# A graph-network kernel: bank and wait value of every visit written out in a 16 bit table instead of packed codes

## Chip, core and metric

One core of a Trainium2 chip. The metric is the device time of one execution in microseconds, the median of the runs shown; lower is better.

## What is computed

Four graph layers follow each other on 3125 nodes with 64 features and 103,125 edges, each behind a layer norm and a ReLU, each added to x. `src` and `dst` are sorted by `dst`. Cut to what matters here:

```python
def reference(x, src, dst, edge_attr_32, edge_attr_64, edge_weight, ...):
    h = relu(layernorm(x)); x = x + L0(h, src, dst)          # 10 hops: segment_sum of (h * norm)[src] by dst
    h = relu(layernorm(x)); x = x + L1(h, (src, dst), edge_weight)   # 3 weighted graph convolutions
    h = relu(layernorm(x)); x = x + L2(h, (src, dst), edge_attr_32)  # attention over edges
    h = relu(layernorm(x)); x = x + L3(h, edge_attr_64, src, dst)    # messages, mean by dst, output
    return x
```

The 13 propagations of L0 and L1 run as products with dense matrices of 3125 x 3125. One of edge counts stays on the chip, one of summed edge weights goes to memory. The change is in how these two matrices are built.

## The kernel before

The program is a row of stages. In each stage every engine has its own instruction stream, and all engines meet at its end. `stage_tables` makes index tables (to 87 us of the profiled execution), `stage_build` builds the two matrices (to about 790 us), then come the hops, the convolutions, attention and messages, which the change leaves as they are.

**Visits.** The 806 tiles of 128 edges (`TB`) meet 392 blocks of 8 destination nodes (`BB`). Because the edges are sorted by `dst`, tiles and blocks are walked together in V0 = 1197 visits: each visit adds one tile's share to one block. For a visit TensorE multiplies one-hot rows (`rows`: source within its 128, once plain and twice times the high and low part of the weight) by one-hot columns (`cols`: node chunk and destination), with 226, 200 and 200 columns (L486, L487, L488). The sums lie in PSUM, the tensor `banks`; block j has bank j mod 8. Visits are made in 120 batches of ten (`TP`) and on TensorE in 240 groups of five (`GV`).

**Who makes what.** VectorE makes the one-hot rows and columns of a batch in five passes: L447, L448, L449 and twice L452. There are two slots for batches, so VectorE begins batch b when all visits up to batch b-2 are done (`vis_done`), and TensorE begins a batch when its one-hots are ready (`oh_ready`). GpSimd copies table values for a batch (L429). ScalarE takes each finished pair of blocks: it copies two banks of sums (L512), zeroes the banks of the pair before (L517, which counts up `freed`), and casts the counts to their place (L519); the pair to take is given by a table of last visits, loaded at L522. SyncE stores the weight sums (L536).

**The codes.** Which bank a visit adds to is known only on the chip. `stage_tables` packs for each group of five visits one 32 bit code: three bits of bank for each visit, and nine bits with the newest block of the group (`JBITS`, `JMAX`, L329 to L339, written to `vis`). In the build stage all 1197 visits are written out for TensorE one after the other, without a loop. Every eighth group (a leg, 40 visits) it loads eight codes into registers (`codes`, L472), each checked against its range. `group` waits for `freed` with a value unpacked from the code (L481), and for each visit takes its bank out by a shift and a mask:

```python
                pe.wait_ge(freed, ((x & (JMAX - 1)) >> 1) + 1)
                for u in range(n):
                    t = GV * half + u
                    bank = (x >> (JBITS + 3 * u)) & (BANKS - 1)
```

These operations on registers are instructions of TensorE's sequencer, which also issues the weight loads and matmuls in program order. The trace names them ALU_OP, FUSED_REGOPS, SEQ_ASSERT (the check) and TENSOR_LOAD (the load of registers).

Of the kernel before, what the change touches and what calls it, by code (L numbers as in the profile page):

```python
# [9 lines left out]
BF16 = mybir.dt.bfloat16  # L10
I32 = mybir.dt.int32
I16 = mybir.dt.int16
ALU = mybir.AluOpType
ACT = mybir.ActivationFunctionType
X = mybir.AxisListType.X
# [25 lines left out]
J0 = NDST // BB  # L41
V0 = T0 + J0 - 1
V0P = 1280
TP = 10
NBATCH = -(-V0 // TP)
GV = 5
NG5 = -(-V0 // GV)
VT = NBATCH * TP
CW = NCH * BB
CAW = CW + NCH + 1  # L50
BANKS = 8
JBITS = 9
JMAX = 1 << JBITS
ROW, COL, CHUNK, WHI, WLO = range(5)
VISW = 640

# [7 lines left out]
GROUP = DC // P  # L64
WDOWN = 2.0 ** -10
NDC = -(-NDST // DC)
BLOCK1, ENDS, BLOCK2 = 0, 32, 96
R = 8
RT = 64
NWORDS = V2P // 4  # L70
# [32 lines left out]
class Mem:  # L103


    def __init__(self, nc, ctx):
# [10 lines left out]

        self.vis = sb("vis", [P, VISW], I16)
        scales = sb("scales", [P, 2], F32)
        self.scale, self.unscale = scales[:, 0:1], scales[:, 1:2]  # L120
        self.ident = sb("ident", [P, P], F32)
        self.iotaH = sb("iotaH", [P, CW], F16)
        self.colsN = sb("colsN", [P, 8, NCH], F32)
# [11 lines left out]
        self.landed_e = [sem(f"landed_e{i}") for i in range(R)]  # L135
        self.landed_q = [sem(f"landed_q{i}") for i in range(R)]

    def steps(self):

        return self.vis[BLOCK1:BLOCK1 + 1, :].bitcast(I32)[:, 0:NG5]  # L140

    def ends(self):

# [2 lines left out]
    def tabs5(self):  # L146

        return self.work[:, 0:5 * VT // 2].bitcast(F16).rearrange("p (k v) -> p k v", k=5)

# [24 lines left out]
def stage_tables(nc, m, last0, last, dst, src, edges):  # L174
# [4 lines left out]
    with ExitStack() as ctx:  # L179
        sem = lambda n: ctx.enter_context(nc.semaphore(n))  # L180
        raw = m.big
        at = [0]

        def take(n):
            at[0] += n
            return raw[:, at[0] - n:at[0]]
# [8 lines left out]
                tI=take(C).bitcast(I32), blkF=take(C), tF=take(C), end=take(C), cmp=take(C * VP // 2).bitcast(BF16).rearrange("p (c v) -> p c v", c=C),  # L195
                tv=take(VP), tvc=take(VP), jv=take(VP + 2), tcol=take(K).bitcast(I32)))
        cmpJ = take(C0 * J0 // 2).bitcast(BF16).rearrange("p (c j) -> p c j", c=C0)
        ends, steps = take(J0), take(NG5)
        r1 = take(K1 * 3 * TB).bitcast(I32).rearrange("p (k a e) -> p k a e", k=K1, a=3)
        r2 = take(K2 * 2 * TE).bitcast(I32).rearrange("p (k a e) -> p k a e", k=K2, a=2)  # L200
        f1 = take(K1 * 4 * TB).rearrange("p (k a e) -> p k a e", k=K1, a=4)
# [3 lines left out]
        valid, tmp = m.work2[:, 0:V0P], m.work2[:, V0P:2 * V0P]  # L205
        jI = m.work2[:, 2 * V0P:3 * V0P].bitcast(I32)
# [12 lines left out]
        for arr in range(4):  # L219
            for k in range(0, K1, 4):  # L220
                n = min(4, K1 - k)
# [16 lines left out]
        def _(po):  # L238
            po.iota(iotaI, pattern=[[1, V0P]], base=0, channel_multiplier=0).then_inc(s_iota, 1)
            for s in schemes:  # L240
                po.iota(s["tI"], pattern=[[P, s["C"]]], base=0, channel_multiplier=1).then_inc(s_iota, 1)
            po.memset(m.ident[:, :], 0.0).then_inc(s_pool, 1)
            po.wait_ge(s_pool, 1)
            po.affine_select(out=m.ident[:, :], in_=m.ident[:, :], compare_op=ALU.not_equal, fill=1.0, base=0,
                             pattern=[[-1, P]], channel_multiplier=1).then_inc(s_iota, 1)
# [46 lines left out]
        def _(dve):  # L292
            chain = m.dve_step.on(dve)
            chain(dve.memset(onesB, 1.0))
            dve.wait_ge(s_iota, 4)
            chain(dve.tensor_copy(iotaF, iotaI))
            chain(dve.tensor_copy(m.iotaH[:, :], iotaI[:, 0:CW]))
            dve.wait_ge(s_last, 32)
            for s in schemes:
                chain(dve.tensor_scalar(s["blkI"], s["lastI"], s["shift"], None, ALU.arith_shift_right))  # L300
                chain(dve.tensor_copy(s["blkF"], s["blkI"]))
                chain(dve.tensor_copy(s["tF"], s["tI"]))
                chain(dve.tensor_tensor(s["end"], s["blkF"], s["tF"], ALU.add))
                for c in range(s["C"]):
                    ins = dve.tensor_scalar(s["cmp"][:, c, :], iotaF[:, 0:s["VP"]], s["end"][:, c:c + 1], None, ALU.is_gt)
                ins.then_inc(s_cmp, 1)
            for c in range(C0):
                ins = dve.tensor_scalar(cmpJ[:, c, :], iotaF[:, 0:J0], schemes[0]["blkF"][:, c:c + 1], None, ALU.is_ge)
            ins.then_inc(s_cmp, 1)
            for n, s in enumerate(schemes):  # L310
                dve.wait_ge(s_tv, n + 1)
                for q in range(s["VP"] // s["chunk"]):
                    part = slice(q * s["chunk"], (q + 1) * s["chunk"])
                    ins = dve.tensor_copy(s["tv"][:, part], m.PB[s["banks"] + q][:, 0:s["chunk"]])
                chain(ins)
                chain(dve.tensor_tensor(s["jv"][:, 1:s["VP"] + 1], iotaF[:, 0:s["VP"]], s["tv"], ALU.subtract))
                dve.tensor_scalar(s["tvc"], s["tv"], float(s["T"] - 1), None, ALU.min).then_inc(s_tvs, 1)
            for n, s in enumerate(schemes):
                dve.wait_ge(s_tc, n + 1)
                for g in range(-(-s["K"] // 4)):  # L320
                    k = min(4, s["K"] - 4 * g)
# [5 lines left out]
            j1 = schemes[0]["jv"][:, 1:V0P + 1]  # L327
            dve.wait_ge(s_tvs, 2)
            chain(dve.tensor_scalar(valid, j1, float(J0 - 1), None, ALU.min))  # L329
            chain(dve.tensor_copy(jI, valid))  # L330
            chain(dve.tensor_scalar(jI, jI, BANKS - 1, None, ALU.bitwise_and))
            chain(dve.tensor_copy(tmp, jI))
            five = tmp[BLOCK1:BLOCK1 + 1, 0:GV * NG5].rearrange("p (k u) -> p k u", u=GV)
            newest = valid[BLOCK1:BLOCK1 + 1, 0:GV * NG5].rearrange("p (k u) -> p k u", u=GV)[:, :, GV - 1]
            code = steps[BLOCK1:BLOCK1 + 1, :]
            chain(dve.scalar_tensor_tensor(code, five[:, :, GV - 1], float(BANKS), five[:, :, GV - 2], ALU.mult, ALU.add))
            for u in range(GV - 3, -1, -1):
                chain(dve.scalar_tensor_tensor(code, code, float(BANKS), five[:, :, u], ALU.mult, ALU.add))
            chain(dve.scalar_tensor_tensor(m.steps(), code, float(JMAX), newest, ALU.mult, ALU.add))  # L339

            dve.wait_ge(s_tv, 3)
            chain(dve.tensor_scalar(ends, m.PB[6][:, 0:J0], float(T0 - 1), 1.0, ALU.min, ALU.add))
# [22 lines left out]
            chain(dve.scalar_tensor_tensor(valid, chT, 1.0, valid, ALU.add, ALU.mult))  # L365
            dve.tensor_scalar(m.tab(COL), tmp[:, 0:VT], -1.0, None, ALU.add)
            dve.tensor_scalar(m.tab(CHUNK), valid[:, 0:VT], -1.0, None, ALU.add)
            chain(dve.tensor_copy(m.tab(ROW), rowT[:, 0:VT]))

# [6 lines left out]
            chain(dve.tensor_scalar(wT, wT, m.scale, None, ALU.mult))  # L376
            chain(dve.tensor_copy(m.tab(WHI), wT[:, 0:VT]))
            chain(dve.tensor_tensor(m.tab(WLO), wT[:, 0:VT], m.tab(WHI), ALU.subtract))

# [14 lines left out]
def stage_build(nc, m, aw):  # L394

    with ExitStack() as ctx:
# [3 lines left out]
        slots = []  # L400
        for home in (m.work[:, free:free + size], m.work2[:, 0:size]):
            h16 = home.bitcast(F16)
            rows = h16[:, 0:3 * TP * P].rearrange("p (i t r) -> p i t r", i=3, t=TP)
# [12 lines left out]
        oh_ready = sem("build_oh")  # L416
        vis_done = sem("build_visit")
        freed = sem("build_freed")
# [5 lines left out]
        @block.gpsimd  # L424
        def _(po):
            for b in range(NBATCH):
                if b >= 2:
                    po.wait_ge(oh_ready, b - 1)
                po.tensor_copy(twice[b % 2], m.tabs5()[:, :, b * TP:(b + 1) * TP].unsqueeze(3).to_broadcast([P, 5, TP, 2])).then_inc(doubled, 1)  # L429

        @block.vector
        def _(dve):
# [5 lines left out]
            def batch(b, k, first=False):  # L438
# [8 lines left out]
                dve.tensor_tensor(pairwise(rows[:, 0, :, :]), iota(P), value(ROW, P), ALU.is_equal).then_inc(rows_ready, 1)  # L447
                dve.tensor_tensor(pairwise(cols[:, :, 0:CW]), iota(CW), value(COL, CW), ALU.is_equal)  # L448
                dve.tensor_tensor(pairwise(cols[:, :, CW:CAW]), iota(CAW - CW), value(CHUNK, CAW - CW), ALU.is_equal)  # L449
                dve.wait_ge(rows_ready, b + 1)  # L450
# [13 lines left out]
            chain = m.dve_step.on(dve)  # L464
            chain(dve.tensor_copy(dout, m.PS[:, 0, 2 * CW:2 * CW + NCH]))
            for b in range(1, BANKS):
                chain(dve.tensor_tensor(dout, dout, m.PS[:, b, 2 * CW:2 * CW + NCH], ALU.add))

        @block.tensor
        def _(pe):  # L470
            def codes(g, n):
                _, xs = nc.values_load_multi_w_load_instructions(m.steps()[:, bass.ds(g, n)], [mybir.EngineType.PE], min_val=0,  # L472
                                                                 max_val=JMAX * BANKS ** GV - 1)
                return xs

            def group(x, b, half, k, n=GV):

                rows, cols = slots[k]
                if half == 0:
                    pe.wait_ge(oh_ready, b + 1)  # L480
                pe.wait_ge(freed, ((x & (JMAX - 1)) >> 1) + 1)  # L481
                for u in range(n):
                    t = GV * half + u
                    bank = (x >> (JBITS + 3 * u)) & (BANKS - 1)
                    to = lambda c0, c1: m.PS[:, bass.ds(bank, 1), c0:c1].rearrange("p b c -> p (b c)")
                    pe.matmul(to(CW, CW + CAW), rows[:, 0, t, :], cols[:, t, :], start=False, stop=True, skip_group_check=True)  # L486
                    pe.matmul(to(0, CW), rows[:, 1, t, :], cols[:, t, 0:CW], start=False, stop=True, skip_group_check=True)  # L487
                    pe.matmul(to(0, CW), rows[:, 2, t, :], cols[:, t, 0:CW], start=False, stop=True, skip_group_check=True).then_inc(vis_done, 1)  # L488

            pe.wait_ge(init, 1)  # L490
            for b in range(BANKS):
                ins = pe.matmul(m.PS[:, b, 0:CW + CAW], blank[:, 0, 0:P], blank.rearrange("p t c -> p (t c)")[:, 0:CW + CAW], start=True, stop=True)
                if b % 2:
                    ins.then_inc(freed, 1)
            for g in range(NG5):
                if g % 8 == 0:
                    xs = codes(g, min(8, NG5 - g))
                group(xs[g % 8], g // 2, g % 2, g // 2 % 2, min(GV, V0 - g * GV))

        @block.scalar  # L500
        def _(act):
# [1673 lines left out]
```

## Time and profile before

| | us |
|---|---|
| median of 3 runs | 3705.48 |
| lowest and highest | 3702.94, 3708.67 |
| the profiled execution, first to last instruction | 4103.0 |
| of it before the build stage | 87 |
| build stage | 703 |
| after it | 3313 |

The profiled execution is 398 us longer than the median of the timed ones. Its rows name engines as PE (TensorE's matmuls), PEld (its weight loads), PEldq (its sequencer), DVE (VectorE), ACT (ScalarE), POOL (GpSimd) and SP (SyncE). Register instructions do not count as busy time; where an engine waited for nothing that the profile can name, the releaser reads "issue". Starts and ends are in us from the first instruction; the ends of matmuls are modelled, their starts are recorded. The granted clock is a share of TensorE's 2.4 GHz, 1.00 or 0.50 at any moment.

### The profile page before, as it was taken

How to read it: one execution, taken by the hardware profiler on the slowest of the kernel's cores; microseconds unless marked ns; L12 is line 12 of the kernel's file. 1: busy time of each engine (PE TensorE's matmuls, PEld its weight loads, DVE VectorE, ACT ScalarE, POOL GpSimd, SP SyncE). 2: the span in 40 equal slices, each digit the busy share in tenths (PEclk: the TensorE clock that was granted, in tenths of full speed). 3: DMA queues.
4: the chain of work that ended last, by engine and by line, in shares of the span. 5: the costliest groups of instructions: out<-in, count | busy, mean ns of one | idle time of the engine just before them, and what ended most of it. 6: DMA issues, size and time to landing. Idle time of an engine off the chain costs nothing. (4 is left out here: it accounts for less than half of the span.)

```text
span 4103.0 us, 80080 instructions
## 1 busy us (share of the span) xinstructions
PE 3139.2 (77%) x17480; PEld 1972.5 (48%) x17480; DVE 1986.4 (48%) x6935; ACT 1606.3 (39%) x4621; POOL 1627.3 (40%) x1766
## 2 busy tenths in 40 slices
PE   3788788879997797577777777777866778787877
PEld 2444444444443343455566656556643444444445
DVE  6656666556656115344444444444673444444442
ACT  1555555413322001233333333333453444444445
POOL 2000000024333001666666666666106666666660
PEclk7899898999998998687777777877977888888885
DMA  1111111125557995322222222222112222222220
GB/s 38 57 59 57 57 59 59 51 93 193 188 177 261 406 360 185 65 54 55 54 55 54 55 54 53 54 55 54 40 28 56 66 63 66 64 66 63 66 61 13
DMA packets 417722, 370.64 MB, mean 90 GB/s; under 512 B 175608, under 2 KB 342232, under 8 KB 417336
## 3 DMA queue, kind: packets, MB, share of 16 engines
q1 hardware_dynamic: 365912, 315.65, 23.8%
q0 software_dynamic: 46144, 48.98, 6.5%
q8 instruction: 198, 3.24, 0.3%
q10 hardware_dynamic: 5280, 1.23, 0.1%
q14 instruction: 188, 1.54, 0.1%
HBM read 279.65 MB, written 86.00 MB: 89 GB/s over the span
## 5 line engine op out<-in xcount | busy, mean ns | idle before, releaser
L1451 POOL DMA_INDIRECT big<-row_table,src x806 | 761.5, 945 | 487.3 <-issue 183.4
L1870 POOL DMA_INDIRECT big<-message_table,src x610 | 612.0, 1003 | 394.5 <-DVE big L2000 172.1
L1476 PE MATMUL banks<-big 97*128 x902 | 399.8, 534 | 148.6 <-issue 138.1
L1492 PE MATMUL banks<-big 128*128 x1804 | 349.0, 326 | 174.8 <-ACT big L1508 110.1
L486 PE MATMUL banks<-work 128*128 128x226 f16 x1197 | 350.3, 293 | 138.6 <-issue 131.0
L1492 PEld LDWEIGHTS banks<-big 128*128 128x128 f32 x1804 | 312.4, 244 | 202.5 <-issue 202.1
L1909 PE MATMUL banks<-big 128*128 128x512 f16 x1225 | 395.6, 441 | 4.4 <-DVE big L1988 4.4
L850 PE MATMUL banks<-big,work 128*128 128x512 f16 (+1 forms) x1750 | 352.1, 359 | 22.3 <-DVE work L984 17.4
L1541 DVE TENSOR_REDUCE big<-banks 128x1 f32<-128x256 f32 x451 | 189.4, 420 | 332.5 <-PE banks L1476 183.8
L1508 ACT COPY big<-banks 128x256 f32<-128x256 f32 x451 | 169.8, 377 | 439.5 <-remote 194.0
L1918 PEld LDWEIGHTS banks<-big 128*64 128x64 f32 x1804 | 173.8, 164 | 343.6 <-issue 343.0
L1918 PE MATMUL banks<-big 128*64 x1804 | 247.5, 268 | 116.5 <-issue 98.3
L487 PE MATMUL banks<-work 128*128 128x200 f16 x1197 | 335.6, 280 | 0.0
L488 PE MATMUL banks<-work 128*128 128x200 f16 x1197 | 326.9, 273 | 0.0
L429 POOL COPY work<-work 128x100 f16<-128x100 f16 x120 | 35.9, 300 | 666.9 <-DVE work L452 649.9
L1558 DVE SCALAR_TENSOR_TENSOR big<-big,banks 128x97 f32 x451 | 142.4, 316 | 325.0 <-remote 208.5
L486 PEld LDWEIGHTS banks<-work 128*128 128x128 f16 x1197 | 121.9, 102 | 363.1 <-issue 350.1
L512 ACT ACTIVATE work<-banks 128x800 f32<-128x800 f32 x196 | 164.3, 838 | 330.6 <-PE banks L488 330.6
L908 POOL TENSOR_TENSOR work<-work 128x400 f16<-128x400 f32 x196 | 180.1, 946 | 284.8 <-DVE work L977 244.2
L2006 DVE TENSOR_SCALAR big<-big 128x512 f16<-128x512 f16 x1225 | 281.6, 285 | 2.3
L2000 DVE TENSOR_TENSOR big<-banks,big 128x128 f32<-128x128 f32 x305 | 87.3, 286 | 399.8 <-remote 257.3
L1476 PEld LDWEIGHTS banks<-big 97*128 97x128 f32 x902 | 177.4, 244 | 198.9 <-issue 196.4
(338 smaller groups left out, 5835.8 us busy)
## 6 DMA issues: line engine op xcount, KB each, us to landing
big<-weights_halves SPq DMA_DIRECT2D x16, 6400.0 KB, 20.8
weights_dense<-work SPq DMA_DIRECT2D x196, 200.0 KB, 1.9
work<-weights_dense SPq DMA_DIRECT2D x196, 200.0 KB, 2.7
weights_halves<-work SPq DMA_DIRECT2D x98, 400.0 KB, 2.6
big<-q_table SPq DMA_DIRECT2D x451, 64.0 KB
big<-in_ef SPq DMA_DIRECT2D x403, 64.0 KB
big<-in_ea SPq DMA_DIRECT2D x403, 32.0 KB
big<-row_table,src POOLq DMA_INDIRECT x806
```

The lines of the kernel that those rows point to most:

```text
L486: pe.matmul(to(CW, CW + CAW), rows[:, 0, t, :], cols[:, t, :], start=False, stop=True, skip_group_check=True)
L487: pe.matmul(to(0, CW), rows[:, 1, t, :], cols[:, t, 0:CW], start=False, stop=True, skip_group_check=True)
L488: pe.matmul(to(0, CW), rows[:, 2, t, :], cols[:, t, 0:CW], start=False, stop=True, skip_group_check=True).then_inc(vis_done, 1)
L850: ins = pe.matmul(m.PB[c % 4][:, 0:width(c)], z[k][:, a, :, :], counts[:, a, c * DC:c * DC + width(c)], start=(a == 0), stop=(a == NCH - 1))
L1451: po.indirect_dma_start(rows[:, t % RT, s, 0:D], None, x_t.rearrange("a p c -> (a p) c"), bass.IndirectOffsetOnAxis(ap=m.src2[:, s, t:t + ...
L1476: pe.matmul(psS[v % 2], qT[v % R][0:XW, :], XF[0:XW, bass.ds(slot, 1), :].rearrange("p t e -> p (t e)"), start=False, stop=True).then_inc( ...
L1492: ins = pe.matmul(psA[v % 2], PT[v % 2][:, s * P:(s + 1) * P], rows[:, bass.ds(slot, 1), s, :].rearrange("p t c -> p (t c)"), start=(s == ...
L1541: dve.tensor_reduce(rm[s3], psS[i % 2], op=ALU.max, axis=X, negate=True).then_inc(s_small, 1)
L1870: po.indirect_dma_start(G[n % R][:, s, :], None, g_t.rearrange("a p c -> (a p) c"), bass.IndirectOffsetOnAxis(ap=m.src2[:, s, t:t + 1], ax ...
L1909: pe.matmul(psH[q % 2], table[:, a, :, :].rearrange("p s d -> p (s d)"), hot[n % HOT], start=(a == 0), stop=(a == NCH - 1)).then_inc(hot_u ...
L1918: ins = pe.matmul(psA[v % 4], oh[v % 4][:, s, :], M[:, bass.ds(slot, 1), s, :].rearrange("p t c -> p (t c)"), start=(s == 0), stop=(s == 1))
L2006: dve.tensor_scalar(hot[n % HOT], key[q % 2], float(P * a - CENTER), None, ALU.is_equal).then_inc(hot_ready, 1)
```

## The change

Instead of one packed code for each five visits, `stage_tables` writes a table of 16 bit numbers. For each leg, now 20 visits, it holds 20 offsets into PSUM (bank times 512) and 4 wait values, one for each group of five, ready for use. 60 legs of 24 numbers lie in two rows of `work` (partitions 0 and 32), in columns that nothing else of the build stage uses. TensorE loads 24 registers a leg with one instruction, with no check of range, adds a constant to the offset for the column, and has no shift, mask or unpacking left.

```diff
+LEG = 2 * TP
+NLEG = VT // LEG
+WALK = LEG + LEG // GV
+WALK_AT = 6160
+BOUNDED = "the table is written from values that are clamped when it is made"
...
+WALK_ROWS = (0, 32)
...
-    def steps(self):
-
-        return self.vis[BLOCK1:BLOCK1 + 1, :].bitcast(I32)[:, 0:NG5]
+    def walk(self, half):
+
+        n = NLEG // 2 * WALK
+        row = WALK_ROWS[half]
+        return self.work[row:row + 1, WALK_AT:WALK_AT + n // 2].bitcast(I16)
+
+    def leg(self, g):
+
+        half, at = divmod(g, NLEG // 2)
+        return self.walk(half)[:, at * WALK:(at + 1) * WALK].bitcast(U16)
...
+            pairI = tmp.bitcast(I32)
             chain(dve.tensor_copy(jI, valid))
+            chain(dve.tensor_scalar(pairI, jI, 1, None, ALU.arith_shift_right))
             chain(dve.tensor_scalar(jI, jI, BANKS - 1, None, ALU.bitwise_and))
-            chain(dve.tensor_copy(tmp, jI))
-            five = tmp[BLOCK1:BLOCK1 + 1, 0:GV * NG5].rearrange("p (k u) -> p k u", u=GV)
-            newest = valid[BLOCK1:BLOCK1 + 1, 0:GV * NG5].rearrange("p (k u) -> p k u", u=GV)[:, :, GV - 1]
-            code = steps[BLOCK1:BLOCK1 + 1, :]
-            chain(dve.scalar_tensor_tensor(code, five[:, :, GV - 1], float(BANKS), five[:, :, GV - 2], ALU.mult, ALU.add))
-            for u in range(GV - 3, -1, -1):
-                chain(dve.scalar_tensor_tensor(code, code, float(BANKS), five[:, :, u], ALU.mult, ALU.add))
-            chain(dve.scalar_tensor_tensor(m.steps(), code, float(JMAX), newest, ALU.mult, ALU.add))
+            n = VT // 2
+            for half, row in enumerate(WALK_ROWS):
+                to = m.walk(half).rearrange("p (g w) -> p g w", w=WALK)
+                part = lambda v: v[row:row + 1, half * n:(half + 1) * n]
+                chain(dve.tensor_scalar(to[:, :, 0:LEG], part(jI).rearrange("p (g v) -> p g v", v=LEG), 512, None, ALU.mult))
+                newest = part(pairI).rearrange("p (g q u) -> p g q u", g=NLEG // 2, u=GV)[:, :, :, GV - 1]
+                chain(dve.tensor_scalar(to[:, :, LEG:WALK], newest, 1, None, ALU.add))
...
+            flat = m.PS[:, :, :].rearrange("p b c -> p (b c)")
+
+            def leg(g):
+                _, xs = nc.values_load_multi_w_load_instructions(m.leg(g), [mybir.EngineType.PE], min_val=0, max_val=(BANKS - 1) * 512,
+                                                                 skip_runtime_bounds_check_because=BOUNDED)
+                return xs[0:LEG], xs[LEG:WALK]
+
+            def batch(b, places, needed):
+
+                rows, cols = slots[b % 2]
+                pe.wait_ge(oh_ready, b + 1)
+                for t in range(min(TP, V0 - b * TP)):
+                    if t % GV == 0:
+                        pe.wait_ge(freed, needed[t // GV])
+                    to = lambda c0, c1: flat[:, bass.ds(places[t] + c0, c1 - c0)]
                     pe.matmul(to(CW, CW + CAW), rows[:, 0, t, :], cols[:, t, :], start=False, stop=True, skip_group_check=True)
...
-            for g in range(NG5):
-                if g % 8 == 0:
-                    xs = codes(g, min(8, NG5 - g))
-                group(xs[g % 8], g // 2, g % 2, g // 2 % 2, min(GV, V0 - g * GV))
+            for g in range(NLEG):
+                places, needed = leg(g)
+                for u in range(2):
+                    batch(2 * g + u, places[u * TP:(u + 1) * TP], needed[u * (TP // GV):(u + 1) * (TP // GV)])
```

TensorE's program where the first leg of the build stage begins, before the change:

```order
L472 TENSOR_LOAD vis
L472 ISA x16
L481 REGISTER_ALU [waits build_oh]
L481 ISA
L486 REGISTER_ALU [waits build_freed]
L486 REGISTER_ALU
L486 ISA
L486 MATMUL banks<-work 128x226
L487 ISA
L487 MATMUL banks<-work 128x200
L488 MATMUL banks<-work 128x200
```

The same place in the changed kernel (L486 is now the load of a leg; L498, L499 and L500 are the three matmuls):

```order
L486 TENSOR_LOAD work
L498 ISA [waits build_freed,build_oh]
L498 MATMUL banks<-work 128x226
L499 ISA
L499 MATMUL banks<-work 128x200
L500 MATMUL banks<-work 128x200
```

The sixteen instructions behind the load, the two of L481 and the two REGISTER_ALU are gone, and both waits stand on one register instruction. There are 30 such loads before and 60 now.

TensorE's program where one group of five ends and the next begins within a batch, before:

```order
L488 MATMUL banks<-work 128x200
L481 REGISTER_ALU
L481 ISA
L486 REGISTER_ALU [waits build_freed]
L486 REGISTER_ALU
L486 ISA
L486 MATMUL banks<-work 128x226
```

and in the changed kernel:

```order
L500 MATMUL banks<-work 128x200
L498 ISA [waits build_freed]
L498 MATMUL banks<-work 128x226
```

Between two visits of one group there are `L486 REGISTER_ALU x2` and `L486 ISA` before, and `L498 ISA` alone now. VectorE's program in `stage_tables`, before:

```order
L332 CAST work<-work 128x1280
L336 SCALAR_TENSOR_TENSOR big<-work 1x240
L338 SCALAR_TENSOR_TENSOR big<-big,work 1x240 x3
L339 SCALAR_TENSOR_TENSOR vis<-big,work 1x240
L342 TENSOR_SCALAR big<-banks 128x392
```

and now:

```order
L344 TENSOR_SCALAR work<-work 128x1280
L349 TENSOR_SCALAR work<-work 1x30x20
L351 TENSOR_SCALAR work<-work 1x30x4
L349 TENSOR_SCALAR work<-work 1x30x20
L351 TENSOR_SCALAR work<-work 1x30x4
L354 TENSOR_SCALAR big<-banks 128x392
```

One pass of a single row less stands there, and the pass over 1280 columns is a mask in place of a cast. The programs of the other engines keep their instructions and their order.

## Rows read from the trace of the kernel before

**Rows 1.** the build stage by engine: busy us (instructions), clock, DMA share, GB/s
```profile
core 0: us, PE busy (x) PEld busy (x) DVE busy (x) ACT busy (x) POOL busy (x), PEclk, DMA share, GB/s
...
87.00:790.00 703.00, 561.62 (x3591) 297.67 (x3591) 430.28 (x602) 395.79 (x587) 35.23 (x118) 0.90 0.16 58
```

**Rows 2.** who waited for whom, 87 to 790: us in all, times, longest
```profile
PEld banks L486 <- issue: 350.1, 958, 3.7
...
DVE work L447 <- PE banks L488: 265.2, 118, 5.3
...
PE banks L486 <- ACT banks L517: 6.2, 24, 0.4
```

**Rows 3.** timeline of TensorE: start and length of loads (PEld) and matmuls (PE)
```profile
400.63 0.10 PEld L486 LDWEIGHTS banks<-work 128*128 128x128 f16 x1 [0.22 <-issue]
...
400.75 0.26 PE L487 MATMUL banks<-work 128*128 128x200 f16 x1
400.76 0.10 PEld L488 LDWEIGHTS banks<-work 128*128 128x128 f16 x1
400.85 0.25 PE L488 MATMUL banks<-work 128*128 128x200 f16 x1
401.08 0.10 PEld L486 LDWEIGHTS banks<-work 128*128 128x128 f16 x1 [0.22 <-issue]
...
402.22 0.25 PE L488 MATMUL banks<-work 128*128 128x200 f16 x1
...
402.82 0.10 PEld L486 LDWEIGHTS banks<-work 128*128 128x128 f16 x1 [0.58 <-issue]
```

**Rows 4.** register instructions of lines 472 and 486: count, ns min/median/max
```profile
L472 PEldq TENSOR_LOAD <-vis x30: 587/591/867, 83.2 to 764.2; - x30
...
L486 PEldq ALU_OP  x2394: 36/36/36, 87.1 to 785.8; - x200
```

**Rows 5.** timeline of TensorE round the load of a leg
```profile
318.69 0.25 PE L488 MATMUL banks<-work 128*128 128x200 f16 x1
322.43 0.36 PE L486 MATMUL banks<-work 128*128 128x226 f16 x1 [3.49 <-issue]
```

**Rows 6.** columns of rows 1, for the 5.5 us behind that load
```profile
322.40:327.90 5.50, 5.47 (x32) 4.54 (x33) 0.28 (x1) 2.97 (x5) 0.27 (x1) 0.50 0.10 37
```

**Rows 7.** other loads of registers: two by line 1230, four by line 522
```profile
L1230 PEldq TENSOR_LOAD <-vis x114: 7/537/727, 1650.6 to 4064.2; - x114
...
L522 ACTq TENSOR_LOAD <-vis x49: 304/307/513, 83.2 to 777.1; - x49
```

**Rows 8.** timeline of VectorE in a batch, then of ScalarE in a pair
```profile
402.59 0.83 DVE L447 TENSOR_TENSOR work<-iotaH,work 128x1280 f16<-128x1280 f16 x1 [1.40 <-PE banks L488]
...
404.65 1.55 DVE L452 TENSOR_TENSOR work<-work 128x1280 f16<-128x1280 f16 x2
...
402.06 0.84 ACT L512 ACTIVATE work<-banks 128x800 f32<-128x800 f32 x1 [1.27 <-PE banks L488]
402.79 0.83 ACT L517 COPY banks<-colsN 128x800 f32<-128x800 f32 x1
403.55 0.53 ACT L519 ACTIVATE big<-work 128x400 f32 x1
```

**Rows 9.** timeline where VectorE's first batch ends and TensorE begins
```profile
85.24 1.55 DVE L452 TENSOR_TENSOR work<-work 128x1280 f16<-128x1280 f16 x2
...
86.71 0.82 DVE L447 TENSOR_TENSOR work<-iotaH,work 128x1280 f16<-128x1280 f16 x1
...
87.42 0.10 PEld L486 LDWEIGHTS banks<-work 128*128 128x128 f16 x1 [1.96 <-issue]
```

**Rows 10.** a group of VectorE ahead of the stage, 20 to 62 us
```profile
L349 DVE TENSOR_SCALAR big<-big 128x128 int32<-128x128 int32 x10 | 2.2, 219 | 12.2 <-DMA big<-in_dst,big 12.0
```

**Rows 11.** the page: instructions in the trace, those of its busy groups
```profile
span 4103.0 us, 80080 instructions
...
PE 3139.2 (77%) x17480; PEld 1972.5 (48%) x17480; DVE 1986.4 (48%) x6935; ACT 1606.3 (39%) x4621; POOL 1627.3 (40%) x1766
```

More of the change, by code:

```diff
@@ L12 @@
 I16 = mybir.dt.int16
+U16 = mybir.dt.uint16
 ALU = mybir.AluOpType
@@ L46 @@
 GV = 5
-NG5 = -(-V0 // GV)
 VT = NBATCH * TP
+LEG = 2 * TP
[3 more added lines that the diff above has]
+BOUNDED = "the table is written from values that are clamped when it is made"
 CW = NCH * BB
@@ L51 @@
 BANKS = 8
-JBITS = 9
-JMAX = 1 << JBITS
 ROW, COL, CHUNK, WHI, WLO = range(5)
@@ L66 @@
 NDC = -(-NDST // DC)
-BLOCK1, ENDS, BLOCK2 = 0, 32, 96
+ENDS, BLOCK2 = 32, 96
+WALK_ROWS = (0, 32)
 R = 8
@@ L197, in stage_tables @@
         cmpJ = take(C0 * J0 // 2).bitcast(BF16).rearrange("p (c j) -> p c j", c=C0)
-        ends, steps = take(J0), take(NG5)
+        ends = take(J0)
         r1 = take(K1 * 3 * TB).bitcast(I32).rearrange("p (k a e) -> p k a e", k=K1, a=3)
@@ L470, in _ @@
         def _(pe):
[L471 to L485, printed above, removed]
+            flat = m.PS[:, :, :].rearrange("p b c -> p (b c)")
[10 more added lines that the diff above has]
+                    to = lambda c0, c1: flat[:, bass.ds(places[t] + c0, c1 - c0)]
                     pe.matmul(to(CW, CW + CAW), rows[:, 0, t, :], cols[:, t, :], start=False, stop=True, skip_group_check=True)
```

## The prediction, made before the changed kernel ran

> **What bounds the kernel now.** Read the stretches first [rows 1]: the build stage, which the change touches, lasts from 87 to 790 us, 703 of 4103 us, and no other stretch runs lines that it edits, except some short passes of VectorE before 87. In the stage no engine is full: VectorE is busy 430 us, ScalarE 396 us, GpSimd 35 us. TensorE reads as busy 562 us, but the ends of its matmuls are modelled. Then the waits of the stage [rows 2]: VectorE waits 265 us for TensorE's L488, and TensorE waits for almost nobody (6.2 us for ScalarE). What stands before L486 is "issue", 350.1 us on the weight loads in 958 pieces, so TensorE's own sequencer sets the pace.
>
> The timeline of single visits shows what it does there [rows 3]. Weight loads of L486 start at 400.63 and 401.08: a visit takes 0.45 us. From the load of L486 to L487, where one register instruction stands, 0.12 us pass; from the load of L488 (400.76) to the next of L486, where three stand (two ALU_OP, one FUSED_REGOPS), 0.32 us. The two ALU_OPs (the shift and the mask, 2394 in all [rows 4]) thus cost 0.32 - 0.12 = 0.20 us a visit. Where a group of five ends, the wait value is unpacked too: from the matmul of L488 to the next load are 0.60 us (402.22 to 402.82) and not 0.23 (400.85 to 401.08), 0.37 more. Where a leg of eight groups ends, the load of eight codes, its sixteen check instructions and the unpacking hold TensorE from a matmul at 318.69 to one at 322.43 [rows 5], 3.74 us.
>
> Together: 957 visits inside groups at 0.465 (0.45, and 0.52 in the slow stretches) are 445 us; 29 pauses at 3.74 are 108 us; the remaining 150 us on 210 group ends are 0.71 each.
>
> **The change part by part, in the time of the profiled execution.**
>
> *Visits.* Without two ALU_OPs the sequencer needs 0.45 - 0.20 = 0.25 us. Now the matmuls themselves count: at the half clock, granted 0.50, 32 matmuls start in 5.5 us [rows 6], a visit of three in 0.52, so they need 0.26 at the full one; the distance of 0.10 from L487 to L488 at full clock [rows 3], where nothing but the matmul holds, gives up to 0.30 for three. I take 0.28: 957 x 0.28 = 268 us.
>
> *Group ends.* The unpacking at L481 goes, and the wait stands on the first register instruction of the group. The wait costs something still: I take 0.1 us over a visit, between nothing and the 0.37 of [rows 3]. 240 x 0.38 = 91 us.
>
> *Loads.* 60 loads of 24 registers replace 30 of eight, without checks. A load of eight took 0.591 us, one of two on the same sequencer 0.537 [rows 4, 7]: 0.009 a register, so 24 make 0.74, with decoding 0.8. The upper bound by rows is ScalarE's 0.307 for four [rows 7], 0.077 each, 1.84 for 24. I take 0.8, because the two rows of TensorE differ so little: 60 x 0.8 = 48 us.
>
> TensorE alone would then need 268 + 91 + 48 = 407 us, 3.4 a batch, in place of 703. It will not be alone.
>
> *VectorE* makes a batch in 3.53 us when nobody holds it: 3.61 from 402.59 to the end of L452 [rows 8], less the 0.08 by which the next batch can overlap it (86.79 and 86.71 [rows 9]). That is 424 us for 120, a floor which the change does not touch. The slots are two, so VectorE's batch b+1 waits for TensorE's b-1 and TensorE's b for VectorE's b. Round that ring two batches cost VectorE's time, TensorE's time and both hand-overs: from the last matmul (402.22, [rows 3]) to VectorE's start at 402.59 are 0.28 us beyond the visit; from VectorE's end at 86.79 to the first weight load at 87.42 were 0.63 [rows 9], of which four of five register instructions go, leaving 0.2. So (3.53 + 3.4 + 0.5) / 2 = 3.7 us a batch, 446 us in all.
>
> *ScalarE* needs 2.02 us for a pair of blocks, 402.06 to 404.08 [rows 8], 396 us for 196. It is below the ring, but only by a tenth, and pairs do not come evenly; with a remainder of slow clock I add 4%: 465 us. The stores take a DMA share of 0.16 [rows 1], which leaves room for a faster stage.
>
> *Clock.* The slow stretches follow the 3.74 us pauses: after the one at 318.69 it is 0.50 from 322.4 to 327.9 [rows 6]. With pauses of at most about a microsecond I expect it near 1, above the 0.90 of [rows 1].
>
> *Tables before the stage.* One pass over 1280 goes for another, and five small ones make way for four; all stand ahead of a wait of 12.0 us for an indirect DMA [rows 10]. They cost nothing; were that cover gone, it would be 1 us either way.
>
> Sum: 703 - 465 = 238 us less in the profiled execution. Behind the stage all engines meet, so it passes on whole.
>
> **From the profiled to the timed execution.** The profiled one took 4103 us, the median is 3705: recording cost 398 us somewhere, and the stage's own share must come off the gain. By span it has 703 / 4103 of it, 68 us. By instructions: the trace has 80,080, of which 48,282 are counted as busy [rows 11]; of the other 31,798, TensorE's sequencer has some 5,750 here (30 x 16, 240 x 2, 1197 x 4), 18%, and double that if half of them elsewhere hide behind others: 144 us. I take 100 us. The timed stage is then about 603 before; after, VectorE's instructions hold it near 453, as few register instructions are left. The gain is 150 us: 3705 - 150 = 3555 us.
>
> **Rivals.**
>
> *Recording costs the stage nothing.* Then the 238 us are whole: 3467 us. For it: matmuls and VectorE's passes look untouched by it. Against it: 398 us must lie somewhere, and register work is what this stage is made of. 15%.
>
> *ScalarE takes the ring.* If freeing a pair of banks comes late for TensorE (the wait at a group's first visit asks for the newest of five blocks), 196 pairs cost 2.02 us plus 0.5 of hand-over, 494 us, and the timed gain is near 110 to 120; with the larger share of recording, 75: 3630 us at the end. For it: a pair's banks come free only behind the 0.84 us pass of the next pair and their own zeroing. Against it: 6.2 us of such waits now. 18%.
>
> *The clock falls and stays.* At 1.2 GHz a batch takes 10 x 0.52 + 0.2 + 0.4 = 5.8 us, 696 us, against 603 timed before: 93 us slower, 3798 us. It decides from the point where a batch passes 5.0 us, that is with the half clock in about seven tenths of the stage. For it: a mean of 0.90 in the stage, so half clock in a fifth of it today. Against it: these stretches follow pauses that go. 4%.
>
> *The load is dear per register.* If 24 registers cost in proportion and not 0.009 us each, the loads grow. By ScalarE's 0.077 [rows 7] a load takes 1.84 us, a batch of TensorE 0.52 more and one round the ring 0.26 more: 31 us, 3586 us, inside the forecast. It ends on the slower side only where TensorE's batch passes 603 / 120 = 5.0 us, 2.8 + 0.2 + 2.0, with a load over 4 us. Rows with eight registers in 0.591 us [rows 4] speak against it: 2%. The Trainium skill, page Runtime: NRT & Kernel Launch, The ~15µs preamble/postamble breakdown and the notes on TENSOR_LOAD, gives about 200 ns a register for loads from HBM, in bulk too; by that a load here would be 4.8 us, the stage 10 x 0.28 + 0.2 + 2.4 = 5.4 us a batch, 648 us, and the kernel 3750. The trace disagrees for this one from SBUF, at 74 ns a register with eight.
>
> *It does not take the two instructions away.* The row of TensorE's order has one in their place; if that one grew to 0.3 us, the time would stand. 2%.
>
> **How the numbers follow.** The forecast, 3500 to 3600, has 57%; the first two rivals 15% and 18%; the last three 8%; 2% for anything else. The range, 3460 to 3635, holds the first three. About 0.2% (7 us) is what a measurement can tell from no change. Faster 0.93, same 0.02, slower 0.05.
>
> **What would show it.** Right: no ALU_OP and no SEQ_ASSERT in the visits; weight loads of L498 0.26 to 0.30 us apart in a batch; a load of some 0.75 us; VectorE's wait at its first operation of a batch down from 265 us to under 50; granted clock near 1; the stage 440 to 500 us in the profile. Wrong: the stage at 470 in the profile and the timed gain far from 150 (then the share of recording was off); ScalarE's zeroing as a releaser of TensorE with tens of us; a clock of 0.5 through whole slices; or a gap of over 1 us at each load.

## The result, and the profile after

The changed kernel takes 3763.74 us (median of 4 runs, 3756.19 to 3768.96) against 3706.15 before: a ratio of 1.015, interval 1.0135 to 1.0164. It is 58 us slower where 150 us less were forecast, and outside the range.

The profiled execution spans 3760.3 us, as long as the timed ones. The build stage lasts from 90 to 842 us, 752 us where [rows 1] had 703. Here is that stretch, in the columns of [rows 1]:

```profile
core 0: us, PE busy (x) PEld busy (x) DVE busy (x) ACT busy (x) POOL busy (x), PEclk, DMA share, GB/s
90.00:842.00 752.00, 455.72 (x3591) 407.82 (x3591) 425.19 (x594) 386.55 (x583) 113.66 (x118) 0.77 0.14 54
```

The same matmuls and the same passes of VectorE as before, but the granted clock is 0.77 and not 0.90. The waits in it (us in all, times, longest), which answer to [rows 2]:

```profile
ACT work L524 <- PE banks L500: 385.6, 126, 30.1
DVE work L459 <- PE banks L500: 319.3, 59, 6.3
PEld banks L498 <- issue: 312.5, 60, 6.3
PE banks L498 <- DVE work L464: 249.7, 51, 5.6
```

The waits of TensorE's weight loads for "issue" were 958, of 350 us in all; now they are 60, of 312 us, up to 6.3 us each. The many small gaps are gone and 60 long ones have come: one for each leg. VectorE waits for TensorE more than before, 319 us for 265. The row with 249.7 us lies inside the same gaps and names VectorE as releaser, but it is not what TensorE waited for: in the trace the first matmul of each of the 60 legs starts behind the end of its load, 0.27 us in the middle, and the one-hots of its batch had then been ready for 2.3 to 4.7 us. The load of a leg, in the columns of [rows 4]:

```profile
L486 PEldq TENSOR_LOAD <-work x60: 5847/6168/6443, 84.7 to 828.2; - x60
```

A load of 24 registers takes 6.17 us, not 0.74. What TensorE does round one of them, the answer to [rows 3] and [rows 5]:

```profile
302.47 0.25 PE L499 MATMUL banks<-work 128*128 128x200 f16 x1
302.56 0.25 PE L500 MATMUL banks<-work 128*128 128x200 f16 x1
302.64 0.26 PE L498 MATMUL banks<-work 128*128 128x226 f16 x1
302.74 0.25 PE L499 MATMUL banks<-work 128*128 128x200 f16 x1
302.82 0.25 PE L500 MATMUL banks<-work 128*128 128x200 f16 x1
307.80 0.37 PE L498 MATMUL banks<-work 128*128 128x226 f16 x1 [4.73 <-DVE work L464]
307.96 0.37 PE L499 MATMUL banks<-work 128*128 128x200 f16 x1
308.13 0.37 PE L500 MATMUL banks<-work 128*128 128x200 f16 x1
308.30 0.40 PE L498 MATMUL banks<-work 128*128 128x226 f16 x1
```

Ahead of the load visits follow each other every 0.27 us, as forecast (L500 at 302.56 and 302.82). Then nothing starts from 302.82 to 307.80. The one-hots that it needs next are ready at 304.12, the end of these two passes of VectorE (two more, which end at 307.72, are for the batch after):

```profile
302.57 1.55 DVE L464 TENSOR_TENSOR work<-work 128x1280 f16<-128x1280 f16 x2
306.17 1.55 DVE L464 TENSOR_TENSOR work<-work 128x1280 f16<-128x1280 f16 x2
```

Behind the pause a visit takes 0.50 us, at half clock:

```profile
307.80:310.40 2.60, 2.60 (x16) 2.21 (x17) 0.00 (x0) 1.34 (x2) 0.25 (x1) 0.50 0.02 6
```

So the shifts and masks did go, and what came in their place costs more: 60 loads of 6.17 us, of which about 1 us each lies beside queued matmuls, and stretches at half clock behind them. In this document a pause is the step from the first matmul of a leg's last visit to the first matmul of the next leg. It holds that visit's own 0.27 us. There are 59 of them here, 321 us in all, 5.4 us each.

### The profile page after: what moved, and what is told of

Its sections match the earlier page's. It is cut to its first block and busy times, and to the rows that moved or that the text cites. A ratio compares the mean times of both kernels' runs of the same rounds, so it can differ in the third digit from the quotient of the medians.

```text
span 3760.3 us, 76875 instructions
## 1 busy us (share of the span) xinstructions
PE 2823.0 (75%) x17480; PEld 1940.9 (52%) x17480; DVE 2035.9 (54%) x6934; ACT 1610.9 (43%) x4621; POOL 1708.0 (45%) x1766
## 5 line engine op out<-in xcount | busy, mean ns | idle before, releaser
L498 PE MATMUL banks<-work 128*128 128x226 f16 x1197 | 378.0, 316 | 298.3 <-DVE work L464 249.7
L1488 PE MATMUL banks<-big 97*128 x902 | 347.1, 470 | 92.2 <-issue 88.9
L441 POOL COPY work<-work 128x100 f16<-128x100 f16 x120 | 115.8, 974 | 640.1 <-DVE work L464 623.0
L499 PE MATMUL banks<-work 128*128 128x200 f16 x1197 | 358.9, 300 | 0.0
L500 PE MATMUL banks<-work 128*128 128x200 f16 x1197 | 356.5, 298 | 0.0
L1921 PE MATMUL banks<-big 128*128 128x512 f16 x1225 | 339.4, 389 | 4.4 <-DVE big L2000 4.4
L2018 DVE TENSOR_SCALAR big<-big 128x512 f16<-128x512 f16 x1225 | 313.3, 310 | 0.4 <-issue 0.2
L498 PEld LDWEIGHTS banks<-work 128*128 128x128 f16 x1197 | 142.7, 119 | 320.6 <-issue 312.5
L1504 PE MATMUL banks<-big 128*128 x1804 | 288.3, 286 | 0.0
L459 DVE TENSOR_TENSOR work<-iotaH,work 128x1280 f16<-128x1280 f16 x120 | 98.6, 822 | 319.3 <-PE banks L500 319.3
L1543 DVE TENSOR_SCALAR big<-big,rel 128x128 bf16<-128x128 f16 x902 | 244.0, 273 | 43.6 <-issue 41.4
L1477 PE MATMUL banks<-ident,big 128*97 128x128 f32 x806 | 188.4, 319 | 99.8 <-DMA big<-row_table,src 87.5
```

The source lines that it names most:

```text
L1488: pe.matmul(psS[v % 2], qT[v % R][0:XW, :], XF[0:XW, bass.ds(slot, 1), :].rearrange("p t e -> p (t e)"), start=False, stop=True).then_inc( ...
L1504: ins = pe.matmul(psA[v % 2], PT[v % 2][:, s * P:(s + 1) * P], rows[:, bass.ds(slot, 1), s, :].rearrange("p t c -> p (t c)"), start=(s == ...
L1543: ins = dve.tensor_scalar(oh[v % 4][:, s, :], iota2, m.rel2[:, s, v:v + 1], -1.0, ALU.is_equal, ALU.add)
L1921: pe.matmul(psH[q % 2], table[:, a, :, :].rearrange("p s d -> p (s d)"), hot[n % HOT], start=(a == 0), stop=(a == NCH - 1)).then_inc(hot_u ...
L2018: dve.tensor_scalar(hot[n % HOT], key[q % 2], float(P * a - CENTER), None, ALU.is_equal).then_inc(hot_ready, 1)
```

## The experiments

All but the first are built from the kernel before or the changed one with a few lines edited. "Stage" is the time from the first matmul of all visits to the last one: 699 us before, 751 us in the changed kernel. The experiments e0, e2, e5, e6, e7 and e10 are single executions.

### Does recording cost 398 us?

The kernel before once more, nothing edited.

> The kernel before once more, for its profile. Question: the profiled execution of before took 4103 us against 3706 timed, that of the changed kernel 3760 against 3764. If recording costs nothing and that one execution was slow in attention and messages alone, this profile spans 3700 to 3710 us, its build stage again near 700, attention near 1100 in place of 1342. If recording costs this kernel 398 us, it spans 4100 again.

The execution with a profile took 3709 us as timed, and its profile spans 3707. Seven executions beside it without one took 3702 to 3713. The build stage (columns of [rows 1]) is as long as it was:

```profile
span 3707.0 us, 80080 instructions
```

```profile
87.00:790.00 703.00, 566.01 (x3596) 297.35 (x3594) 431.52 (x599) 394.20 (x585) 32.67 (x118) 0.89 0.16 58
```

Recording costs nothing that shows. Attention takes 1094 us from the first matmul of its L1473 to the last where the first profile had 1342, messages 767 from the first of L1909 to the last where it had 927: 408 us together, so the whole difference of the spans (396 us) lies there and none in the build stage. In a later set of runs on another chip the kernel before took 4106 to 4115 us timed, and the profiles of that set, of edited kernels, have attention at 1344 to 1348 us and messages at 927. The first profile then was most likely taken on such a chip. Why a chip is slower there is not shown. In each experiment below the kernel before was timed on the same chip as the edited one.

### Is it the table's width, or the number of registers?

The changed kernel with 32 bit words. They need four rows in place of two, and the wait value is masked once a group (cut to the lines that matter):

```diff
-WALK_ROWS = (0, 32)
+WALK_ROWS = (0, 32, 64, 96)
...
-        return self.work[row:row + 1, WALK_AT:WALK_AT + n // 2].bitcast(I16)
+        return self.work[row:row + 1, WALK_AT:WALK_AT + n].bitcast(I32)
...
-                        pe.wait_ge(freed, needed[t // GV])
+                        pe.wait_ge(freed, needed[t // GV] & 1023)
```

> The changed kernel with its table in 32 bit words (four rows of 15 legs) and still 24 registers a load; the wait value is masked once a group, 240 instructions of about 0.1 us. Theory A, a 16 bit number is dear to load (0.257 us a register, 6.17 us for 24) and a word is not: the load falls to 0.7 to 0.8 us, the build stage from 752 to 450 to 500, the kernel to 3450 to 3520. Theory B, the number of registers in one load is what costs, whatever their width: the load stays at 6 us, the stage at 740 to 760, the kernel at 3760.

3463.06 us (3459.62 to 3466.96), ratio to before 0.934 (0.932 to 0.935). The stage takes 452 us. Load, stretch and waits:

```profile
L486 PEldq TENSOR_LOAD <-work x60: 1612/1844/1923, 85.2 to 534.3; - x60
```

```profile
89.00:541.00 452.00, 348.16 (x3590) 284.29 (x3591) 427.93 (x595) 381.45 (x581) 84.26 (x118) 1.00 0.24 89
```

```profile
PEld banks L498 <- issue: 128.2, 104, 2.1
ACT work L524 <- PE banks L500: 88.7, 76, 26.3
PE banks L498 <- ACT banks L529: 43.9, 27, 1.9
PE banks L498 <- DVE work L464: 42.3, 34, 1.8
PE banks L498 <- issue: 17.3, 10, 1.8
DVE work L459 <- PE banks L500: 13.1, 31, 1.0
```

Words are cheap to load and 16 bit numbers are dear, with as many registers. The load is 1.84 us, though, not the 0.74 forecast: 24 times 0.077. The clock stays at 1.00 through the stage, and VectorE waits 13 us for TensorE where it waited 319: it is busy 428 of 452 us. This run alone cannot tell the width from everything else that came with it, the four rows above all; e11_words24_shifted below does.

Run again beside another experiment below it gave 3465.08, ratio 0.935 (0.934 to 0.937).

> e1_words24 once more on the same chip as its shifted twin: load 1.6 to 1.9 us, stage 452 us, 0.934 of before where before takes 3706 us.

### Does a shorter leg of 16 bit numbers help?

```diff
-LEG = 2 * TP
+LEG = TP
...
-                for u in range(2):
-                    batch(2 * g + u, ...
+                for u in range(1):
+                    batch(g + u, ...
```

> The changed kernel with legs of one batch: 120 loads of 12 registers of 16 bits in place of 60 of 24. Theory A, each register of 16 bits costs 0.257 us: a load takes 3.1 us, the sum of all loads stays at 370 us, the stage 700 to 770. Theory B in the form that only registers beyond eight are slow (5.6 us for 16, 0.35 each): a load takes 2.0 us, the sum 240 us, the stage falls to 620 to 660.

3720.75 us, where before takes 3707.08. A load of 12 takes half of what one of 24 takes, so the cost is per register from the first one on, 0.26 us; registers beyond eight are no dearer.

```profile
L486 PEldq TENSOR_LOAD <-work x120: 2859/3122/3426, 83.5 to 792.0; - x120
```

```profile
87.00:797.00 710.00, 437.24 (x3585) 366.32 (x3586) 429.15 (x596) 388.38 (x581) 45.40 (x118) 0.85 0.15 57
```

The sum of the loads is the same (120 x 3.12 = 374 us, 60 x 6.17 = 370) and nearly that of TensorE's pauses (119 of 2.8 us, 331 us, and 59 of 5.4 us, 321 us; beyond the visit of 0.27 in each, 299 and 305), yet the stage is 40 us shorter: the clock is 0.85 and not 0.77. Half clock was granted for 217 us and not for 346, and of the visits within legs 338 and not 501 took about 0.51 us in place of 0.27, which is some 40 us. More but shorter pauses cost less in clock here.

### What does the check of the codes cost?

The kernel before, with `skip_runtime_bounds_check_because` on its load of codes and nothing else.

> The kernel before with packed codes, shifts and masks kept, but the codes loaded without the check: the 16 check instructions behind each of 30 loads go. By the rows of before they take 8 x 0.28 = 2.3 us of each 3.74 us pause: 65 to 75 us less, kernel 3630 to 3645. If the pauses were hidden behind another engine: no change, 3706.

3643.98 us (3638.66 to 3644.86), ratio 0.982 (0.980 to 0.984), 63 us less, 2 us short of what was expected. The pauses at the legs' ends, measured as above, fall from 3.7 to 1.4 us each, and the clock rises from 0.90 to 0.99:

```profile
89.00:722.00 633.00, 540.25 (x3588) 253.03 (x3588) 429.36 (x595) 392.63 (x583) 32.63 (x118) 0.99 0.17 64
```

This part of the change is good by itself. TensorE's sequencer still sets the pace there, 0.45 us a visit at full clock.

### The other way round: words, with the check

`skip_runtime_bounds_check_because` taken out of e1_words24, and the mask of the wait value with it.

> As e1_words24 (words, 24 a load) but with the check of each of the 24 registers, 48 instructions a load. A check took 0.28 us in the kernel before, so a leg stands for 1.84 + 24 x 0.28 = 8.6 us, longer than in the changed kernel, with half clock behind it: 60 x (8.6 + 20 x 0.27 + some 3 of slow clock) = 1020 us, less what VectorE and the queue hide; stage 850 to 1000 against 452. If checks ran beside the matmuls: 450 to 500.

3911.78 us on a chip where before took 3705.69; the stage takes 896 us.

```profile
90.00:986.00 896.00, 450.83 (x3557) 403.00 (x3558) 425.89 (x594) 383.77 (x577) 106.07 (x117) 0.72 0.12 45
```

With one number a register instead of five visits a word, there are six times the registers, 1440 for 240, and a check for each. The loads are as short as in e1_words24 (1.84 us), but a pause is 7.9 us and not 2.1, 0.24 us more for each of the 24 checks. With the check this table costs 206 us where without it it saves 244.

### How does the price of a load go with its length?

Words in legs of one batch, 12 a load: the edit of e2_half12 on e1_words24.

> As e1_words24, but legs of one batch: 120 loads of 12 words in place of 60 of 24. If a word costs 0.077 us (24 in 1.84), a load takes 0.92 us and the sum is the same 110 us: stage 445 to 460, kernel 3455 to 3470. If words come in pieces of eight at 0.55 to 0.6 us each (2 words took 0.537, 8 took 0.591, 24 between 1.61 and 1.9), 12 words take 1.1 to 1.2 us, the sum is 140 us, and the stage 450 to 475, kernel 3460 to 3490.

This ran where before takes 4110.81 us: 3868.37, ratio 0.941 (0.939 to 0.942), 242 us less, as e1_words24 on its chip (244 us less). The stage is 453 us.

```profile
L486 PEldq TENSOR_LOAD <-work x120: 844/852/1147, 83.3 to 537.3; - x120
```

12 words take 0.85 us (the median; two fifths of the loads take 0.15 to 0.3 us more, which nothing here explains), 24 between 1.6 and 1.9, 8 take 0.59: a straight line through nothing, and no pieces of eight. Off it lie two words at 0.537 [rows 7]. Two kernels with packed codes, unchecked, load six and three words at a time (`g % 8` and `min(8, ...)` with 6 or 3 in the place of 8):

> As e3_codes_unchecked (packed codes, no check), but six words a load, 40 loads. Loads so far: 4 words 0.307 us, 8 0.591, 12 0.852, 24 1.61 to 1.9, but 2 words 0.537, and 16 bit numbers 0.257 each. Theory C, four neighbouring words come together for 0.3 us and anything else comes one at a time for 0.26: six words take 0.3 + 2 x 0.26 = 0.83 us. Theory D, 0.075 us a word, the two-word load being something else: 0.45 us.

> As e6_codes6, three words a load, 80 loads. Theory C, no four together: 3 x 0.26 = 0.78 us a load, 62 us in all against 18 in e3_codes_unchecked, stage about 665 to 680 against 633. Theory D: 0.23 us a load, 18 us in all, the stage as in e3_codes_unchecked, 625 to 640.

```profile
L472 PEldq TENSOR_LOAD <-vis x40: 814/1284/1758, 83.3 to 733.9; - x40
```

```profile
L472 PEldq TENSOR_LOAD <-vis x80: 762/768/1038, 83.5 to 759.7; - x80
```

Three words take 0.77 us, more than eight: 0.256 a word. Six take 0.81 to 0.83 us in most of every second load (0.87 to 1.10 in four of these 20) and 1.47 to 1.76 in the others. The cheap loads begin at a multiple of 48 bytes, counted from the start of the row, the dear ones 24 bytes on, which is no multiple of 16. The loads of e4_words12 begin at every multiple of 48, so a multiple of 16 is enough. The rule that fits all of them: four words come together for about 0.3 us if the load begins at a multiple of 16 bytes; what is left over, and everything in a load that begins elsewhere, comes one by one for 0.25 to 0.26. The stages are 662 and 679 us (633 in e3_codes_unchecked), the kernels 3678 and 3686 us. The loads take 49 and 65 us in all where those of e3_codes_unchecked took 19, 30 and 46 us more, and the stages grow by 29 and 46.

### Then is it the width at all?

e1_words24 with its table one word, 4 bytes, further on, not an instruction more or less:

```diff
-WALK_AT = 6160
+WALK_AT = 6161
```

> As e1_words24, but the table of words begins one word further on in its rows (column 6161 in place of 6160); no instruction more or less. Theory C as e6_codes6 shows it (six words from a place divisible by four words took 0.82 us, from another place 1.47): only a load that begins at a multiple of 16 bytes takes four words at once, any other takes each word alone. Then 24 words here take 24 x 0.257 = 6.2 us like the 16 bit numbers of the changed kernel, the stage 740 to 760 us, and the kernel is 1.5% slower than before. If the width of 16 bits is what costs: load 1.85 us, stage 452, 6.6% faster than before. If four are taken from the next multiple on: 1 + 5 x 4 + 3 words, 2.5 to 2.8 us, stage 480 to 520.

3762.72 us (3755.11 to 3769.20), ratio 1.016 (1.014 to 1.018), beside e1_words24 at 0.935 on the same chip.

```profile
L486 PEldq TENSOR_LOAD <-work x60: 5858/6158/6517, 83.0 to 823.8; - x60
```

```profile
90.00:842.00 752.00, 454.88 (x3589) 406.68 (x3587) 425.25 (x602) 390.54 (x588) 114.29 (x117) 0.77 0.15 54
```

The stretch is the one shown for the changed kernel; from the first matmul to the last the stage has 747 us, 751 there, with words of 32 bits. One word of displacement costs 298 us. The number of rows is the same as in e1_words24, so it is not what made that kernel fast. Words from such a place cost what 16 bit numbers cost, 0.257 us each, though those of the changed kernel begin at a multiple of 16 bytes. So 16 bits cost, it seems, because such numbers are taken one by one from any place; that they are is read from this price and not seen directly.

### Who is late next?

e1_words24 with VectorE's second pass of L464 left out from the third batch on, so that the low part of the weights is that of the first two batches:

```diff
-                for i, kind in ((1, WHI), (2, WLO)):
+                for i, kind in ((1, WHI), (2, WLO))[:2 if first else 1]:
```

> As e1_words24, but from the third batch on VectorE leaves out the second pass of L464 (the low part of the weights, which then stays that of the first two batches, so the output is not the reference's). VectorE's batch falls from 3.53 to 2.8 us. If VectorE alone bounds the stage of e1_words24 (452 us, VectorE waits 21 us in it), the stage falls by 80 us to 370, the kernel to 3380. If TensorE is as near (1197 x 0.268 + 60 x 1.7 = 423 us), the stage falls only to 425 to 440, the kernel to 3435 to 3455.

The stage is 442 us, 10 less, for 88 us less work on VectorE. The kernel takes 3863.90 us on the chip with 4110.81, ratio 0.940 (0.939 to 0.942), 4.5 us less than e4_words12 there.

```profile
89.00:531.00 442.00, 342.32 (x3580) 285.31 (x3578) 339.61 (x474) 381.90 (x584) 62.66 (x117) 1.00 0.25 91
```

```profile
DVE work L459 <- PE banks L500: 97.5, 60, 2.2
```

VectorE now waits 98 us: TensorE with its loads of 1.84 us is nearly as late as VectorE was, and the stage ends a little above the 425 to 440 us expected for that case. Then e1_words24 with the loads doubled, so that TensorE's sequencer stands twice as long:

```diff
-                places, needed = leg(g)
+                places, _ = leg(g)
+                _, needed = leg(g)
```

> As e1_words24, but each leg is loaded twice (offsets from one load, wait values from the other), so TensorE's sequencer stands for 3.7 us a leg in place of 1.84. If the pause of the sequencer is what made the changed kernel slow, whatever the table's width: TensorE is the bound, 60 x 1.84 = 110 us more, less about 30 us of slack, and the granted clock falls behind pauses as it did behind those of 3.74 us before: stage 540 to 620, kernel 3550 to 3630, VectorE's wait for TensorE over 80 us. If the loads lie beside VectorE's work: no change, 3463.

3987.78 us where before takes 4110.81; the stage 571 us and the clock 0.86.

```profile
89.00:661.00 572.00, 410.87 (x3591) 364.60 (x3589) 427.17 (x595) 385.51 (x583) 79.42 (x118) 0.86 0.19 71
```

60 more loads of 1.84 us are 110 us, and the stage grows by 119. About half of that is longer pauses, 3.2 us for 2.1, 61 us in all. The clock gives some 70 us: 308 visits within legs take 0.51 us. A few short waits within the legs of e1_words24 are gone. At the loads of e1_words24 hardly anything is slack any more.

## Why the prediction was wrong, point by point

**What bounds the kernel** was read rightly. TensorE's sequencer sets the pace of the stage before; e1_words24, which takes its work away, shortens it by 247 us.

**Visits.** Right: 0.28 us forecast, 0.27 measured, the two ALU_OPs gone and no gap left between visits.

**Group ends.** 0.1 us was put on each; in the changed kernel a visit at a group's end takes 0.27 us at full clock like the others, so some 24 us too much.

**Loads: the step that failed.** It put 60 x 0.8 = 48 us for them. They take 60 x 6.17 = 370 us, of which 305 us stand in TensorE's pauses beyond the 0.27 us of a visit in each. The price per register was the difference of two rows, two words at 0.537 and eight at 0.591, 0.009 a register. Those two loads are of different kinds: two words taken one by one (0.268 each), and eight in two fours (0.30 each). ScalarE's four words in 0.307 [rows 7], of the same kind as the eight, were kept as an upper bound only; the line through them, 0.075 a word, is that of e1_words24 and e4_words12. But no row of before would have given the 0.257 for 16 bit numbers unless the 0.537 had been read as twice 0.268. The form of the loaded numbers changed with the change, from words to half words, and the text never asked what that does. Its own sign of being wrong, a gap of over 1 us at each load, is what the profile shows.

**The rival that came true** is the dear load, held for 2%. The Trainium skill (Runtime: NRT & Kernel Launch, Instruction fetch mechanics, note on TENSOR_LOAD) has about 200 ns a register, for loads from HBM. The trace has 257 ns for these from on-chip memory, and 74 to 77 ns for words in fours. By the page's price the prediction had 3750 us; measured are 3764. That the two are so near is luck: its stage was 648 us against a timed 603 before, and both are some 100 us short of the measured 751 and 699. The load was a fifth too cheap, the clock was left out, and the share taken for recording, which does not exist, hid it in the difference. The prediction let one row, 74 ns a register with eight words, speak against a dear load; that row is for fours.

**Clock.** "With pauses of at most about a microsecond I expect it near 1" is right: 1.00 in e1_words24, even with pauses of 2.1 us, and 0.77 with pauses of five, the case that it left out. In the changed kernel 346 of 751 us were granted at half clock, before 145 of 699; 501 visits took 0.51 us and not 0.27, 122 us more. The stage adds up from that: 1196 steps of 0.27 are 323 us, the pauses beyond them 305, the slow visits 122, together 750. Slow visits cost 40% of the pauses here, 27% in e2_half12 and in e5_words24_checked, 43% in e10_load_twice.

**VectorE's floor and the ring.** The forecast's formula, with 1197 x 0.27 + 60 x 1.84 = 434 us for TensorE (3.6 a batch), gives (3.53 + 3.6 + 0.5) / 2 = 3.8 us a batch, 458 us; e1_words24 has 452 at clock 1.00. The 4% added for ScalarE and the clock were not needed. The formula is no more than a rough guide, though: with VectorE's 2.8 us of e8_one_pass_less it gives 414 us and the stage has 442, nearer to the 434 of TensorE alone. ScalarE as a third bound shows with 44 us of waits in e1_words24 and 48 in e10_load_twice, which is the most. That the 465 us forecast lie near the 452 of e1_words24 is partly luck: even for words the loads were 62 us too low, visits and group ends some 34 us too high, the formula passes on half of what is left, and the 4% (19 us) covers it.

**From profiled to timed.** The 398 us were no cost of recording, and none of them lay in the stage. Taking 100 us off the gain was the second step that failed: with cheap loads the gain is 242 to 244 us, near the 238 of the rival that left recording out (3467 us, measured 3463 and 3465). A span that differs from the timed median by a tenth has to be compared stage by stage with a second profile; from one profile alone the cause could not be told.

**The tables ahead of the stage** cost nothing that shows: the first visit starts at 90.8 us, behind a first load of 5.8 us, and at 87.4 and 89.6 in the two profiles of the kernel before.

So the direction failed on one term, 370 us for 48, and on the clock that hangs on it. The list of rivals had it but held it for unlikely.

## What to carry to other kernels

Loading registers from on-chip memory is work of the sequencer, and here all but about 1 us of each 6.17 us load left TensorE without work; count it by its elements and look where they begin. Four 32 bit words from a place divisible by 16 bytes took about 0.3 us here, hardly more than one element alone (0.26), so a table for registers is best made of words, in multiples of four, and aligned: in this kernel the place alone is worth 298 of 3465 us. When a change alters the type, the length or the place of what an instruction reads, rows of the old form do not price it; put a chance on the new form being another case.

## What the hardware showed that was not expected

- A load of registers by TensorE's sequencer: 16 bit numbers 0.257 us each (12 in 3.12 us, 24 in 6.17); words from a place divisible by 16 bytes 0.07 to 0.077 us each in fours (8 in 0.59, 12 in 0.85, 24 in 1.61 to 1.9), and 0.25 to 0.26 each otherwise (3 in 0.77, 24 in 6.16). The places are counted from the start of the row of the tensor.
- The half clock follows pauses of TensorE. With 59 pauses of 7.9 us each (e5_words24_checked) 55% of the stage was at half clock, of 5.4 us (the changed kernel) 46%, of 3.2 us (e10_load_twice) 29%, of 2.1 us (e1_words24) and of 1.3 us (e4_words12, 119 of them) about 1% or less. The length of the pauses alone does not decide it: e7_codes3, where visits are 0.45 us apart and not 0.27, has 79 pauses of 1.6 us and 10% of its stage at half clock.
- Chips differ: the kernel before took 3706 to 3707 us on three of the chips in these runs and 4111 us on one. The edited kernels profiled there have the difference in attention and messages.
